# 16-head cross attention: the inverse denominators are spread to all partitions by a store and a stride-zero load instead of by TensorE, and the divisions come later in the next batch

## The reference

```python
# HEADS = 16, DIM_HEAD = 64, x is (16, 100, 128), context is (16, 1444, 96)
q, k, v = x @ Wq, context @ Wk, context @ Wv       # each split in 16 heads of 64
attn = softmax(q @ k^T * 64 ** -0.5, axis=-1)       # 100 x 1444 per batch and head
out = concat_heads(attn @ v) @ Wo + bo              # added to x
```

## Time and profile before

| what | value |
|---|---|
| median of 3 runs | 4973.12 us |
| lowest and highest | 4944.28, 4980.82 us |
| the profiled execution's own time | 4966.12 us |
| its span, first to last instruction | 4964.2 us |
| busy TensorE, VectorE, ScalarE, GpSimd | 86%, 56%, 40%, 33% of the span |
| the 16 batches of this attention | about 262 to 1480 us of the span |

### The profile page before, as it was taken

One profiled execution on the slowest core, in us unless ns is written; L12 is line 12 of the kernel. 1 busy time (PEld: TensorE's weight loads), 2 busy tenths in 40 slices (PEclk: granted clock), 3 DMA queues, 4 the chain that ended last, 5 costly groups with the idle time before them and its releaser, 6 DMA issues. The chain is left out here.

```text
span 4964.2 us, 88758 instructions
## 1 busy us (share of the span) xinstructions
PE 4246.6 (86%) x27918; PEld 2986.8 (60%) x27918; DVE 2781.1 (56%) x4307; ACT 1978.0 (40%) x3118; POOL 1662.4 (33%) x1320
## 2 busy tenths in 40 slices
PE   8899999999998988967879999999695666756799
PEld 4578888888876855834445555555353444444477
DVE  4344454454433443545634666665536999987433
ACT  2255555555542223213423455454233444440222
POOL 2255666666643323102421113230032343320042
PEclk8799999999997989979955899998796888878699
DMA  2000000000001210420011223221001011100021
GB/s 88 1 10 19 10 19 10 19 19 10 19 1 40 61 25 19 109 64 17 2 33 34 58 56 67 55 58 40 0 2 36 23 32 28 28 16 0 1 64 48
DMA packets 124783, 154.03 MB, mean 31 GB/s; under 512 B 86928, under 2 KB 110240, under 8 KB 124224
## 3 DMA queue, kind: packets, MB, share of 16 engines
q1 hardware_dynamic: 124352, 148.54, 12.0%
HBM read 110.25 MB, written 2.66 MB: 23 GB/s over the span
## 5 line engine op out<-in xcount | busy, mean ns | idle before, releaser
L1046 POOL TENSOR_TENSOR pexp_lo<-arena,pexp_hi 128x800 fp32r<-128x800 f32 x384 | 636.2, 1657 | 435.8 <-POOLq L1045 435.8
L2381 DVE TENSOR_REDUCE arena<-ps 100x1 f32<-100x482 f32 (+1 forms) x768 | 490.7, 657 | 287.9 <-DVEq L2368 278.8
L2261 DVE TENSOR_REDUCE arena<-ps 128x1 f32<-128x482 f32 (+3 forms) x624 | 392.9, 656 | 361.4 <-DVEq L2239 351.4
L1529 ACT ACTIVATE arena<-ps 128x800 f32<-128x800 f32 x384 | 322.1, 839 | 495.9 <-ACTq L1527 493.7
L3300 PE MATMUL ps<-kst,qs 96*100 96x482 f32 (+1 forms) x768 | 389.1, 509 | 41.1 <-PEq L3254 37.7
L1629 ACT ACTIVATE arena<-ps 128x800 f32<-128x800 f32 x384 | 315.4, 836 | 260.7 <-ACTq L1628 260.4
L992 POOL TENSOR_TENSOR max_diag<-w_const,arena 100x800 fp32r<-100x800 f32 x160 | 246.7, 1542 | 448.3 <-POOLq L990 448.3
L2573 DVE MATCH_REPLACE8 arena<-arena 128x1444 f32<-128x1444 f32 x208 | 340.8, 1645 | 0.0
L1530 ACT ACTIVATE pexp_hi<-ps 128x800 fp32r<-128x800 f32 x384 | 319.6, 832 | 0.0
L2675 DVE TENSOR_TENSOR arena<-ps,arena 128x400 f32<-128x400 f32 x256 | 147.0, 574 | 282.1 <-DVEq L2674 282.1
L2034 DVE TENSOR_REDUCE arena<-ps 100x8 f32<-100x800 f32 x160 | 158.2, 991 | 259.2 <-DVEq L2031 259.2
(11 more groups left out here) (396 smaller groups left out, 9535.9 us busy)
## 6 DMA issues: line engine op xcount, KB each, us to landing
ctxT<-in_ctxT SPq DMA_DIRECT2D x56, 541.5 KB
kst<-mid SPq DMA_DIRECT2D x128, 180.5 KB, 3.1
ctxk<-in_ctx SPq DMA_DIRECT2D x40, 528.0 KB
chunk<-in_ff_chunks SPq DMA_DIRECT2D x77, 193.0 KB, 2.4
arena<-gate_dram SPq DMA_DIRECT2D x64, 200.0 KB, 3.9
kst<-xn SPq DMA_DIRECT2D x64, 180.5 KB, 2.9
arena<-gate_dram SPq DMA_DIRECT2D x64, 100.0 KB, 2.6
arena<-in_ctxT SPq DMA_DIRECT2D x8, 541.5 KB
```

Source lines behind the costliest of these rows:

```text
L1046: own(nc.gpsimd.tensor_tensor(pexp_lo[p % 3][:, :, :], pexp[p % 3], pexp_hi[p % 3][:, :, :], ALU.subtract))
L1529: nc.scalar.activation(pexp[p % 3], of, ACT.Exp, scale=scale).then_inc(s.pexp_ready, 1)
L2261: peak = nc.vector.tensor_reduce(mparts[0:at.stop - at.start, m, c:c + 1], bank(k, z - a, at.stop - at.start), AX.X, ALU.max)
L2381: peak = nc.vector.tensor_reduce(mparts2[:, h, c:c + 1], bank(k, z - a, S), AX.X, ALU.max)
```

## The change

In all batches but the last, the inverses are no longer spread by TensorE. VectorE inverts `den_rows` in step 3 as before and signals `rexp_ready`; SyncE, which waits for that behind the issue of the next context load, stores `den_rows` to a row of 1600 numbers in DRAM, waits for the store, and loads that row with a stride of zero to all 97 partitions of `rexp`, which now has 97 partitions in place of 16. VectorE multiplies u by it in steps 15, 16, 17 and 18 ("divide"), with both operands in SBUF, and TensorE projects in step 19 in place of 12. The division after the last batch is as before.

```diff
-    rexp = shared([HEADS, HEADS, S])
+    rexp = shared([C + 1, HEADS, S])
...
+    den_dram = nc.dram_tensor("den_dram", (1, HEADS * S), F32).ap()
...
         if tail:
-            items += {3: [("recips", 0, 0)], 4: [("recips", 1, 0)], 5: [("spread", 0, 0)], 6: [("spread", 1, 0)],
-                      7: [("spread", 2, 0)], 11: [("spread", 3, 0)], 12: [("project", 0, 0)]}.get(p, [])
+            items += {3: [("inverses", 0, 0)], 15: [("divide", 0, 0)], 16: [("divide", 1, 0)], 17: [("divide", 2, 0)],
+                      18: [("divide", 3, 0)], 19: [("project", 0, 0)]}.get(p, [])
...
+            def spread_inverses():
+                sp.wait_ge(s.rexp_ready, 1)
+                sp.sem_inc(s.rexp_ready, -1)
+                sp.dma_start(den_dram.rearrange("o (h t) -> (o h) t", t=S), den_rows[:, :]).then_inc(s.scratch_stored, 16)
+                sp.wait_ge(s.scratch_stored, 16)
+                sp.sem_inc(s.scratch_stored, -16)
+                sp.dma_start(rexp.rearrange("p h t -> p (h t)"), den_dram.to_broadcast([C + 1, HEADS * S])).then_inc(s.den_loaded, 16)
...
                 for par in range(2):
                     denominators(par)
                     load_context(2 * i + 2 + par, par)
+                    spread_inverses()
             denominators(0)
+            spread_inverses()
             denominators(1)
...
+            def invert():
+                dve.wait_ge(s.den_loaded, 16)
+                dve.sem_inc(s.den_loaded, -16)
+                dve.wait_ge(s.u_raw_ready, 1)
+                dve.sem_inc(s.u_raw_ready, -1)
+                nc.vector.reciprocal(den_rows[:, :], den_rows[:, :]).then_inc(s.dve_done, 1)
+                dve.wait_ge(s.dve_done, 1)
+                dve.sem_inc(s.dve_done, -1)
...
+                elif kind == "inverses":
+                    invert()
+                    dve.sem_inc(s.rexp_ready, 1)
+                elif kind == "divide":
+                    if arg == 0:
+                        dve.wait_ge(s.den_loaded, 16)
+                        dve.sem_inc(s.den_loaded, -16)
+                    hs = u[1 - par][:, 4 * arg:4 * arg + 4, :]
+                    nc.vector.tensor_tensor(hs, rexp[:, 4 * arg:4 * arg + 4, :], hs, ALU.mult).then_inc(s.dve_done, 1)
                     dve.wait_ge(s.dve_done, 1)
                     dve.sem_inc(s.dve_done, -1)
+                    dve.sem_inc(s.u_ready, 1)
```

More of the change, by code:

```diff
@@ L2288, in side @@
                 elif kind == "recips" and arg == 0:
[L2289 to L2293, removed]
+                    invert()
+                elif kind == "inverses":
+                    invert()
+                    dve.sem_inc(s.rexp_ready, 1)
[5 more added lines that the diff above has]
+                    nc.vector.tensor_tensor(hs, rexp[:, 4 * arg:4 * arg + 4, :], hs, ALU.mult).then_inc(s.dve_done, 1)
                     dve.wait_ge(s.dve_done, 1)
                     dve.sem_inc(s.dve_done, -1)
+                    dve.sem_inc(s.u_ready, 1)
                 elif kind == "recips":
-                    nc.vector.tensor_tensor(rexp, den_rows[:, :].unsqueeze(1).to_broadcast([HEADS, HEADS, S]),
+                    nc.vector.tensor_tensor(rexp[0:HEADS], den_rows[:, :].unsqueeze(1).to_broadcast([HEADS, HEADS, S]),
                                             W("const", "ident")[0:HEADS, 0:HEADS].unsqueeze(2).to_broadcast([HEADS, HEADS, S]),
@@ L3113, in side @@
             def side(kind, arg, b, par, ahead):
-                if kind in ("recips", "rows"):
+                if kind in ("recips", "inverses", "divide", "rows"):
                     return
@@ L3142, in side @@
                     k = side_bank()
-                    ins = mm(bank(k, GT, C + 1), W("const", "ones")[0:HEADS, 0:C + 1], rexp[:, 4 * arg:4 * arg + 4, :], start=True, stop=True)
+                    ins = mm(bank(k, GT, C + 1), W("const", "ones")[0:HEADS, 0:C + 1], rexp[0:HEADS, 4 * arg:4 * arg + 4, :], start=True, stop=True)
                 else:
@@ L3201, in batch @@
                 for p in range(4 * PAIRS):
-                    items = [it for it in sides_at(p, prep, tail) if it[0] not in ("rows", "recips")]
+                    items = [it for it in sides_at(p, prep, tail) if it[0] not in ("rows", "inverses", "divide")]
                     values(p, par)
```

## The result

The changed kernel takes 4921.82 us, the median of 20 runs, against 4955.57 us for 20 runs of the kernel before: 34 us less. The ratio, 0.9922 with a 95% interval of [0.9898, 0.9946], is taken over the executions in the faster of two states alone and makes 39 us. 4936 was forecast as 30 us under the profiled execution of before.

A forecast was written before the change was run, and what follows sets the result against it. TensorE, busy 299.0 of 300 us, was taken as the bound. Spreads save 4.11 us per batch, 2.2 return as waits, 1.9 stay: 15 x 1.9 = 28.5; 4966 - 28.5 - 1 = 4936 us, range 4901 to 4968.

The forecast's parts named there:

- What the spreads cost: TensorE's spreads in steps 5, 6, 7 and 11: removing them saves 4.11 us per batch, 61.7 us over 15 batches.
- What comes back: TensorE waits for ScalarE in steps 7 and 8 and GpSimd in step 15: 2.2 us of the 4.11 lost again.
- The walk: One batch followed without spreads: TensorE at step 7 at 581.83, held until 582.68 by ScalarE's exponents, 0.85 us lost.
- The project: TensorE's project takes 3.74 us, the same in step 19 as in 12, where it let GpSimd catch up.
- The divide: VectorE's multiplies in steps 15 to 18, 0.57 us each, exclude GpSimd's subtractions; nothing taken on the path.
- rival B: Steps 15 to 18: each divide holds GpSimd 0.57 us on TensorE's path, subtractions 2.2 us; 4970 us; chance 0.14.
- The spread load: DMA load of 97 x 6400 bytes into `rexp`: 12 us, bounds 2 and 21, hidden before the divide of step 15.
- Rival D: The spread load is late and VectorE stands at step 15; needs over 27 us for the load; chance 0.02.
- The sum: Whole kernel: 4966 less 28.5 for 15 batches at 1.9 us and 1 for the last batch's wait, 4936 us.
- the last one's wait: Last batch: TensorE's 1.46 us wait, where VectorE's multiply stood behind GpSimd, goes; counted as 1 us.

The follow-up runs named there:

- e11: e5 with ScalarE's rounding of the value side in step 12 in place of 11; 72.04 us per batch, ratio 0.9910 to the kernel before.
- e4: The changed kernel with GpSimd's low parts spread over steps 6, 8, 10, 12 and 14, 16, 18, 20; 73.01 us per batch, ratio 0.9901.
- e5: The changed kernel with ScalarE's rounding in steps 4, 9, 11 and GpSimd's low parts in 10, 12, 14, 16 and 18 to 21; 72.40 us per batch.
- e1: The kernel before with TensorE's spreads kept but moved to steps 15 to 18 and the project to 19; 78.43 us per batch, ratio 1.0047.
- e7: The changed kernel with VectorE's four multiplies left out, sums undivided; 73.78 us per batch, ratio 0.9975.
- e6: The changed kernel with each of VectorE's four multiplies done twice, first into a spare tile; 80.16 us per batch, ratio 1.0141.
- e2: The changed kernel with the divides in steps 9 to 12 and the project in step 13; 84.88 us per batch, ratio 1.0271.

## Why the prediction was right

- **What the spreads cost.** 4.11 us per batch were forecast from step lengths. e11, with the waits gone, shows 75.94 - 72.04 = 3.90, and the last batch, which never had them, about 3.9 too. Not all of the 4.11 was the spreads': step 5's 4.05 us hold a wait ahead of the spread (0.21 us recorded), for `rexp`. Their recorded durations alone (8 passes of 531 ns, 4.2 us) would have come close by accident: for the neighbours, recorded durations are almost twice what they take.
- **What comes back.** 2.2 us were forecast, 1.1 for ScalarE in steps 7 and 8 and 1.1 to 1.2 for GpSimd in step 15. Measured: 1.4 in steps 5 to 8, which begins two steps earlier than I walked it, and 0.8 in step 15. The sum in this batch, 2.2, is that forecast; over all batches it is 73.86 - 72.04 = 1.8. The walk had TensorE at step 7 unhindered, while the exponents of step 6, behind the rounding of step 5, were late already. That the waits hang on ScalarE's and GpSimd's own work is shown by moving it (e4, e5, e11), and by e1, where they come up without the change.
- **The project.** 3.74 us forecast. Step 19 takes 6.10 us against 2.60 before (623.50 to 626.10 in the batch of the earlier trace rows), so 3.50; step 12 keeps 3.50 where I had 3.25. I had taken step 13 for step 12 without the project, and it is 0.3 us shorter; the two errors cancel.
- **The divide.** Nothing on the path was forecast, and e7 shows 0.08 us. GpSimd's subtractions take 1.72 us at most in all batches, where rival B needed 2.2. That it was so close to costing much was not seen: my bound of 2.5 us of GpSimd against a step of 2.6 to 3.0 is the right comparison for GpSimd, but in e6 the one that breaks is VectorE's. The single meeting of 1.80 us in step 5 is gone: GpSimd's subtraction there takes 1.60.
- **The spread load.** Here the prediction was wrong and lucky. It took 12 us with an upper bound of 21, by scaling a 128-partition load; it takes 26, outside the bounds. Rival D needed a load of over 27 us and was given a chance of 0.02. e2, with the divides 6 steps earlier, is that rival come true: 9 us more per batch than before the change. How many engines a load of 97 rows gets was not looked at.
- **The sum.** 28.5 us for the 15 batches and 1 for the last one's wait were forecast; 35 were measured in this attention, and 34 to 39 in the total with an interval of 12 us either way. What was missed is the last batch: it was priced like the others, 1.9 us and the 1, and gave 5.4, because there the waits don't come back. 4936 itself is 14 us above the measured 4921.82, and 10.5 of these are the 4966.12 it starts from, which lies that much above the median of 20 runs; that the errors of the parts stay small in the total is partly luck.

## What to carry to other kernels

Work taken off the bounding engine pays only until the engine that was covered by it is late: walk the steps behind the cut, with each feeder's rhythm, and spread the feeders' bursts before or with the cut (here 2 us of 4 per batch came back, and moving the side work of ScalarE and GpSimd to other steps regained 1.8 of them in this attention). A batch without that side work, as the last one here, shows what the cut is worth without the waits. Look at the number of rows of a DMA as at its bytes: here 128 rows, of which 31 are never read, took a sixth of the time of 97. Where VectorE and GpSimd exclude each other, count the gaps between GpSimd's instructions and their length: here one multiply per gap was free, and a second one mostly waited for the next gap.

## What the runs showed of the hardware

- A load of one DRAM row to 97 partitions ran on one of 16 DMA engines at 26 GB/s, 26 us for 606 KB; to 128 partitions 800 KB took 4.2 us.
- What the exclusion of VectorE's two-operand multiply and GpSimd's subtraction costs doesn't grow in step with the work: four multiplies per batch cost 0.08 us, eight cost about 5 at a granted clock of 1.00 and 6.3 in the mean, and in one batch under 1.
- When TensorE stood still for 9 us in e2, the granted clock of that stretch fell: 0.68 and 0.50 in two stretches of 4 us, and 0.50 is the lower of its two levels, 1.2 of 2.4 GHz. Behind the wait it was 0.54 for 4 us more. In e6 it fell to 0.62 and 0.52 behind waits of 0.2, 1.4, 0.6 and 1.8 us in four steps. In the changed kernel, with its waits of 0.2 to 0.6 us, it stayed at 1.00.

```profile
368.00:372.00 4.00, 0.00 (x0) 0.00 (x0) 0.00 (x0) 0.00 (x0) 3.00 (x3) 0.68 0.07 28
372.00:376.00 4.00, 0.41 (x1) 0.39 (x2) 1.79 (x4) 0.00 (x0) 1.34 (x2) 0.50 0.02 8
```
